# Second half of a 16-expert layer: down products from one fp32 product to three passes on split operands

## What is computed

```python
weights, indices = _gate(x2, Wg)          # four of sixteen experts for a token
for e in range(16):
    we = jnp.sum(weights * (indices == e), axis=-1)
    h = silu(x2 @ W1[e].T + b1[e]) * (x2 @ W3[e].T + b3[e])
    y = y + (h @ W2[e].T + b2[e]) * we[:, None]
x = x + tanh(g_ffn[2]) * y
```

## Time and profile before

| | |
|---|---|
| median of 3 runs (lowest, highest) | 599.43 us (598.75, 601.22) |
| the profiled execution's own time | 601.89 us |
| its span from first to last instruction | 600.1 us |
| busy in the span: PE, DVE, ACT, POOL | 94%, 75%, 69%, 17% |
| share of PE on the chain that ended last | 71% |
| layer 2's loop of 32 steps, in the span | 387.2 to 449.5 us |

### The profile page before, as it was taken

The page is one execution under the profiler, slowest core; times in us unless marked ns, Lnnn a source line. Parts: engine busy times, 40 slices in busy tenths (PEclk is TensorE's granted clock), DMA queues, the critical chain, the costliest instruction groups (busy, mean ns, idle before and its releaser), DMA issues.

```text
span 600.1 us, 8818 instructions
## 1 busy us (share of the span) xinstructions
PE 566.8 (94%) x3305; PEld 394.1 (66%) x3310; DVE 447.4 (75%) x696; ACT 415.2 (69%) x579; POOL 103.8 (17%) x69
## 2 busy tenths in 40 slices
PE   7999999989999999999896989999998999999997
PEld 5688787656677777775230436566545777888886
DVE  4378987588657898987989676766766847787786
ACT  4798999756755556647999765534513858888885
POOL 5400000001200000003989703200000210000000
PEclk9999999999999999999999799999998999999999
DMA  6207210200200811020000024505510110812100
GB/s 237 71 12 307 71 35 2 74 2 2 76 0 4 317 55 58 2 70 1 5 1 1 1 71 120 164 2 153 163 35 2 37 37 0 301 52 72 37 0 35
DMA packets 16782, 40.27 MB, mean 67 GB/s; under 512 B 1834, under 2 KB 6058, under 8 KB 16740
## 3 DMA queue, kind: packets, MB, share of 16 engines
q1 hardware_dynamic: 16740, 39.71, 19.9%
HBM read 39.01 MB, written 0.70 MB: 66 GB/s over the span
## 4 chain that ended last, share of the span: by engine, by line
PE 71%; DVE 14%; ACT 10%; issue 3%; POOL 1%; DVEq 0%; ACTq 0%; POOLq 0%
PE ps L713 38%; ACT work L1094 6%; PE ps L756 4%; PE ps L452 3%; DVE h_lo L1609 2%; PE ps L469 2%; PE ps L739 2%; PE ps L584 2%; PE ps L741 2%; PE ps L555 2%; PE ps L740 2%; PE ps L569 2%; PE ps L459 2%; PE ps L695 2%; DVE h_act L1586 1%
## 5 line engine op out<-in xcount | busy, mean ns | idle before, releaser
L1609 DVE TENSOR_TENSOR h_lo<-h_act,h_hi 128x512 fp32r<-128x512 f32 (+1 forms) x136 | 118.4, 874 | 39.8 <-ACT h_hi L1139 39.0
L713 PE MATMUL ps<-n_hi,w_hi 128*128 128x512 f32 (+1 forms) x232 | 85.4, 402 | 2.0 <-DVE h_act L1586 1.3
L1139 ACT CAST h_hi<-h_act 128x1024 fp32r<-128x1024 f32 (+1 forms) x88 | 75.3, 856 | 14.6 <-PE ps L713 12.1
L713 PE MATMUL ps<-n_hi,w_lo 128*128 128x512 f32 (+1 forms) x232 | 83.0, 391 | 0.0
L713 PE MATMUL ps<-n_lo,w_hi 128*128 128x512 f32 (+1 forms) x232 | 83.0, 391 | 0.0
L1817 POOL TENSOR_TENSOR rstd<-var_eps,minus_half 128x4 f32<-128x4 f32 x16 | 17.5, 1093 | 319.4 <-DVE var_eps L1273 319.4
L713 PE MATMUL ps<-h_hi,w_hi 128*128 128x512 f32 (+1 forms) x184 | 65.5, 398 | 0.1
L713 PE MATMUL ps<-h_hi,w_lo 128*128 128x512 f32 (+1 forms) x184 | 64.0, 390 | 0.0
L713 PE MATMUL ps<-h_lo,w_hi 128*128 128x512 f32 (+1 forms) x184 | 63.9, 389 | 0.0
L1094 ACT ACTIVATE work<-work,p_rest 128x2048 f32<-128x2048 f32 x31 | 59.5, 1998 | 0.4 <-DVE work L1468 0.4
L1132 ACT ACTIVATE h_act<-ps 128x512 f32<-128x512 f32 (+1 forms) x48 | 28.6, 596 | 40.4 <-PE ps L713 40.4
(11 more groups left out here) (234 smaller groups left out, 1023.7 us busy)
## 6 DMA issues: line engine op xcount, KB each, us to landing
work<-g_rows SPq DMA_DIRECT2D x36, 512.0 KB, 6.4
w_f<-in_w SPq DMA_DIRECT2D x20, 512.0 KB, 3.6
w_f<-in_w SPq DMA_DIRECT2D x8, 544.0 KB, 3.6
work<-in_w SPq DMA_DIRECT2D x2, 512.0 KB, 4.3
work<-g_rows SPq DMA_DIRECT2D x4, 256.0 KB, 9.7
p_rest<-in_p_rest SPq DMA_DIRECT2D x1, 714.0 KB, 9.8
p_attn<-in_p_attn SPq DMA_DIRECT2D x1, 546.5 KB, 6.9
x<-in_xT SPq DMA_DIRECT2D x1, 512.0 KB, 3.6
```

The lines of the kernel that those rows point to most:

```text
L713: mm = pe.matmul(dst[i], wap(wt, e, lo, size, rows), mv[i], start=(first and c == 0), stop=(last and c == 2))
L1139: act.copy(places(h_hi, m, step), places(h_act, m, step)).then_inc(s["hi"], 1)
L1609: dve.tensor_tensor(lo, src, hi.bitcast(F32), ALU.subtract).then_inc(s["lo"], 1)
```

## The change

The downs of steps 16 to 31 (`t == 1`) are made as the ups are: three passes on split operands in place of one fp32 product. For that, ACT rounds each scaled result to a high part (`high2`, one CAST of 128 x 512), DVE subtracts to get the low part (`low2`), and W2 is split in four pieces of four experts each (`split_hi_down2` on ACT, `split_lo_down2` on DVE). The parts of steps 16 to 25 have two buffers, taken in turn (`spare` for the high part, the first halves of `n_hi` and `n_lo` for the low part), so `high2(step)` waits for down step - 2; steps 26 to 29 have four more in `h_hi`, `h_lo`, and steps 30, 31 take the first two again.

`ahead_of` now goes one up for two downs from step 3 on, until four ups are ahead, and then one for one. DVE's products follow `products2`. Where the other work stands is changed too: the norm's mean, variance, spread and the queries after downs 20, 23, 26 and 29; its square and copy on ACT inside the loop; the key copies at ACT's steps 18 and 19; the keys spread one piece a step. The small `uv_line` is now a piece of `h_act`.

```diff
     def ahead_of(self, step):
+        if self.layer == 2:
+            return min(max(min(step + self.ahead + 1, 18 + max(step - 3, 0) // 2), step + 5), self.total)
...
+        def h2_split(step):
+            if 26 <= step < 30:
+                return [flat(h)[:, (step - 26) * HALF:(step - 25) * HALF] for h in (h_hi, h_lo)]
+            return spare[:, half(step % 2)], (n_hi, n_lo)[step % 2][:, 0:HALF]
+        def products2(step):
+            m = MOES[2]
+            return min(m.ahead_of(step) - (2 if step < 8 else 3) if step < 27 else step + 3, m.total)
...
-                        pe.wait_ge(s["scaled"], step + 1)
-                        pe.matmul(ps[:, acc + t], down2(e), h_part[step % 16], start=False, stop=(step + 1 == m.last_of(t))).then_inc(s["h_used"], 1)
+                        if t == 0:
+                            pe.wait_ge(s["scaled"], step + 1)
+                            mm = pe.matmul(ps[:, acc], down2(e), h_part[step % 16], start=False, stop=(step + 1 == m.last_of(t)))
+                        else:
+                            pe.wait_ge(s["lo"], step - 15)
+                            if e % 4 == 0:
+                                pe.wait_ge(s["wld"], e // 4 + 1)
+                            hi, lo = h2_split(step)
+                            pe.matmul(ps[:, acc + 1], down2_half(w_hi, e), hi, start=False, stop=False)
+                            pe.matmul(ps[:, acc + 1], down2_half(w_hi, e), lo, start=False, stop=False)
+                            mm = pe.matmul(ps[:, acc + 1], down2_half(w_lo, e), hi, start=False, stop=(step + 1 == m.last_of(t)))
+                        mm.then_inc(s["h_used"], 1)
...
+                def high2(step):
+                    act.wait_ge(s["scaled"], step + 1)
+                    if step < 26:
+                        act.wait_ge(s["h_used"], step - 1)
+                    else:
+                        act.wait_ge(s["hid"], 2 * (step - 13) if step < 30 else m.total)
+                        act.wait_ge(s["h_used"], 26)
+                    act.copy(h2_split(step)[0], h_part[step % 16]).then_inc(s["hi"], 1)
...
+                        if step == 27:
+                            norm_square(6, 0)
+                            norm_copy(6, 0)
+                        for ready in range(16, m.total):
+                            if min(products2(min(ready + 1, m.total - 1)), m.total - 1) == step:
+                                high2(ready)
...
+                def low2(step):
+                    dve.wait_ge(s["hi"], step - 15)
+                    dve.tensor_tensor(h2_split(step)[1], h_part[step % 16], h2_split(step)[0].bitcast(F32), ALU.subtract).then_inc(s["lo"], 1)
...
-                        if step + 12 < m.total:
+                        while len(made) < products2(step):
                             ahead()
                         scale(step)
+                        if step >= 17:
+                            low2(step - 1)
+                        if step in (11, 15, 19, 23):
+                            split_lo_down2((step - 11) // 4)
```

More of the change, by code:

```diff
@@ L143, in flamingo @@
         uv = sb("uv", [P, 2, S])
-        uv_line = sb("uv_line", [2, T])
+        spare = sb("spare", [P, T], F32R)
         uv_rows = nc.dram_tensor("uv_rows", (2, T), F32, kind="Internal").ap()
@@ L153, in flamingo @@
         h_lo = sb("h_lo", [P, 2, T], F32R)
+        uv_line = h_act[0:2, 0]
         g_sb = sb("g_sb", [P, 2, T])
@@ L242, in up2_lo, with down2_half, four, down2_four @@
             return cols(w_lo if e < 8 else flat(h_lo), e, 2 * P)
+        def down2_half(w, e):
+            return w[:, e * P:(e + 1) * P]
+        def four(w, g):
+            return w[:, 4 * g * P:4 * (g + 1) * P]
+        def down2_four(g):
+            return (w_f32[:, T + g * HALF:T + (g + 1) * HALF] if g < 2 else diag[:, (g - 2) * HALF:(g - 1) * HALF])
+        def h2_split(step):
[5 more added lines that the diff above has]
+            return min(m.ahead_of(step) - (2 if step < 8 else 3) if step < 27 else step + 3, m.total)
         def down2(e):
@@ L266, in flamingo @@
         mo = [{k: sem(f"m{m.layer}_{k}") for k in ["hid", "act", "h_used", "whu", "wlu"] + ["mul"] * m.gated
-              + ["wlu_first"] + (["scaled", "sel"] if m.layer == 2 else ["hi", "lo", "whd", "wld", "wld_first", "gate", "acc"]) + ["xn"] * (m.layer == 3)} for m in MOES]
+              + ["wlu_first"] + (["scaled", "sel", "hi", "lo", "whd", "wld"] if m.layer == 2 else ["hi", "lo", "whd", "wld", "wld_first", "gate", "acc"]) + ["xn"] * (m.layer == 3)} for m in MOES]
         w_in = [[sem(f"w{m.layer}_in{u}") for u in range(m.slots if m.layer != 2 else 0)] for m in MOES]
@@ L903, in _ @@
             moe(MOES[1], {42: [lambda: norm_mean(4, 0)], 43: [lambda: norm_var(4, 0)], 44: [lambda: norm_spread(4, 0)], 46: [first_features]})
-            moe(MOES[2], {19: [lambda: norm_mean(6, 0)], 21: [lambda: norm_var(6, 0)], 24: [lambda: norm_spread(6, 0)], 28: [lambda: queries(1, 0)]})
+            moe(MOES[2], {20: [lambda: norm_mean(6, 0)], 23: [lambda: norm_var(6, 0)], 26: [lambda: norm_spread(6, 0)], 29: [lambda: queries(1, 0)]})
             attention(1)
@@ L1146, in high, with split_hi_down2 @@
                     act.copy(h_hi[0:size, (step % 4) // 2, half(step % 2)], src).then_inc(s["hi"], 1)
+                def high2(step):
[6 more added lines that the diff above has]
+                    act.copy(h2_split(step)[0], h_part[step % 16]).then_inc(s["hi"], 1)
+                def split_hi_down2(g):
+                    act.wait_ge(w2_down_in[g // 2], 16)
+                    act.copy(four(w_hi, g), down2_four(g)).then_inc(s["whd"], 1)
                 def copy_gates(t=0):
@@ L1161, in moe @@
                 if L == 2:
+                    act.wait_ge(pre["uv_dram"], 16)
                     copy_gates(0)
@@ L1193, in moe @@
                             copy_gates(1)
-                        if step in (19, 22):
-                            copy_keys(1, 1, (step - 19) // 3)
-                        for t in range(2):
-                            if step - 23 - 5 * t in (0, 1):
-                                for h in range(2):
-                                    expand_keys(1, t, 2 * (step - 23 - 5 * t) + h)
+                        if step in (18, 19):
+                            copy_keys(1, 1, step - 18)
+                        if step in (17, 20, 22, 24):
+                            split_hi_down2((17, 20, 22, 24).index(step))
+                        if 20 <= step < 28:
+                            expand_keys(1, (step - 20) // 4, step % 4)
+                        if step == 27:
[4 more added lines that the diff above has]
+                                high2(ready)
                     load_table(ACT.Exp)
-                    norm_square(6, 0)
-                    norm_copy(6, 0)
                     query_rows(1, 0)
@@ L1598, in scale, with split_lo_down2 @@
                     dve.tensor_tensor(h, h, g_half[:, e], ALU.mult).then_inc(s["scaled"], 1)
+                def low2(step):
+                    dve.wait_ge(s["hi"], step - 15)
+                    dve.tensor_tensor(h2_split(step)[1], h_part[step % 16], h2_split(step)[0].bitcast(F32), ALU.subtract).then_inc(s["lo"], 1)
+                def split_lo_down2(g):
+                    dve.wait_ge(s["whd"], g + 1)
+                    dve.tensor_tensor(four(w_lo, g), down2_four(g), four(w_hi, g).bitcast(F32), ALU.subtract).then_inc(s["wld"], 1)
                 def low(step):
@@ L1648, in moe @@
                 if L == 2:
-                    steps = itertools.count()
+                    made = []
                     def ahead():
-                        product(next(steps))
+                        made.append(len(made))
+                        product(made[-1])
                     def add(t):
@@ L1692, in moe @@
                             add(0)
+                    low2(m.total - 1)
                     query_rows(1, 0)
@@ L1804, in _ @@
             pair_sums()
[L1805 removed]
+            moe(MOES[2], {**rotations(1, 4), 24: [lambda: norm_eps(6, 0)], 28: [lambda: norm_out(6, 0)]})
             attention(1)
```

5 lines of the change are left out of this document (2 added, 3 removed).

## The result

The changed kernel takes 616.6 us (median of five executions, 615.5 to 621.2), the kernel before 599.3 us beside it. The ratio is 1.029, with a 95% interval of 1.026 to 1.032. A sixth execution of the changed kernel was disturbed (1950.61 us) and is left out of all of this; with it the median would be 618.2. The profiled execution took 619.72 us for a span of 617.9, against 601.89 and 600.1.

A forecast was written before the change was run, and what follows sets the result against it. PE was taken to bound layer 2. Savings (-2.1 + 0.7 - 0.4) and 15.5 us of waits made 13.7; with 1.5 for the clock, +15.2 on 599.4 gave 614.6 us, range 607.5 to 620.

The forecast's parts named there:

- up 24: Second half: PE waits 2.3 us for product 22, behind rounding, low part and sum that follow down 15.
- Saved: Up to the queries: thirteen downs at 0.70 us in place of 0.86, -2.1; down 29 adds 0.7; a 0.44 gap goes.
- up 20: PE waits 1.2 us for product 18, which stands behind DVE's key turn and ACT's second key copy.
- up 25: PE waits 1.7 us for product 23, behind low part 19, whose rounding waits for down 17's buffer.
- the variance: Layer norm: PE waits 1.4 us for ACT's square, which stands behind hidden 27 and a spread of keys.
- downs 26 and 27: Loop's end: each right behind an up (30, 31) that its high and low parts hang on; 2.2 us wait each.
- down 29: Last down ahead of the queries: a wait of 0.5 us at the loop's end.
- The walk: Stepping through the new in-order engine lists with the old trace's prices, noting PE's waits: 15.5 us; queries 13.7 us later.
- The clock: In the stretch with ten gaps, one fall of PE's clock, counted at 1.5 us; none and three were the ends.
- The rival with several falls: Layer 2's loop: the clock falls three times or more, +18.2 us and up, 617.6 to 622 us; chance 0.14.
- PE does not wait: Rival for the whole loop: engines run far enough ahead; 1.8 us less, 597.6 us; chance 0.06.
- Only the end waits: Rival: places 1 to 4 of the waits vanish, 6.7 us at the end stay; +4.9, 604.3 us; chance 0.08.

The follow-up runs named there:

- e4: e1's order, unsplit, with the second half's downs in three passes on operands that lie ready, so no rounding or subtraction for them; 604.1 us, 1.008 of the kernel before.
- e10: e8 with another searched order, GpSimd's power and hand-overs counted longer, and the first two roundings waiting for no down; 596.8 us, 0.9945 of the kernel before.
- e9: The kernel before, nothing split, with its PE, ACT and DVE lists from down 3 to the scores put in a searched order; 598.3 us, 0.996.
- e1: The changed kernel's order with nothing split: all down products single fp32 products, no roundings or low parts; 606.8 us, 1.012 of the kernel before.
- e6: The changed kernel with the ups running five steps ahead of the downs in the second half in place of four; 612.4 us, 1.018 of the kernel before.
- e8: The changed kernel's split and two buffers, with PE, ACT and DVE lists from down 3 in a searched order and some waits freed; 597.4 us, 0.995 of before.
- e2: The changed kernel with idle products on PE ahead of its longest waits, no wait taken away; 615.0 us, 1.024 of the kernel before.
- e7: The changed kernel with a third buffer for high parts of steps 16 to 25, roundings 26 to 29 not waiting for down 25; 615.6 us, 1.026 of before.

## Why the prediction held, and where it was off

The time lay in the range (607.5 to 620), 2.0 us above the forecast of 614.6; one of the five executions, 621.2, lies above the range. Two terms of the sum were off, in opposite directions: the waits were somewhat smaller than forecast, and the clock cost more.

**What bounds, and the prices.** Held. Two downs of three passes start 0.70 us apart; the five ups that waited for DVE started 0.05 or 0.06 us after their product's record ended, and not the 0.15 of the earlier trace rows. But behind such a first pass the next one starts 0.33 us later and not 0.23, so what a hand-over costs PE is some 0.15 after all. For up 24 (the weight load is engine PEld):

```profile
423.66 0.19 PEld L763 LDWEIGHTS ps<-n_hi,h_hi 128*128 128x128 f32 x1 [2.49 <-DVE y_g L1639]
423.99 0.39 PE L764 MATMUL ps<-n_lo,h_hi 128*128 128x512 f32 x1
424.22 0.40 PE L765 MATMUL ps<-n_hi,h_lo 128*128 128x512 f32 x1
```

The row is no clean price of a product's hand-over: the weight load of that up waited too, and the profile puts it down to GpSimd, which made the weights' low part.

```profile
385.67 0.19 PEld L739 LDWEIGHTS ps<-n_hi,h_hi 128*128 128x128 f32 x1 [0.89 <-POOL h_lo L1833]
```

The Trainium skill (TensorE: Matmul & The Clock Gate, section "Architectural detail: the array is 16× 32×32, not 1× 128×128") says that PE's queue can pull weight loads ahead of running matmuls. At this hand-over the trace does not show it: the first weight load of up 24 stands at 423.66 with its pass, and not in the 2.06 us of wait ahead of it.

**Saved.** 0.16 us for a down were forecast, 2.6 for the sixteen in the stretch. PE's work there is less by 2.2 us (the estimate above), in e4, where the clock did not fall, by 2.3, and in e10 against e9, where nothing waits, by 2.9. Held.

**Added waits.** The places were right, all but the last: up 20 1.2 forecast and 1.14 measured; up 24 2.3 and 2.06; up 25 1.7 and 0.87, up 26 0.8 and 0.60; the variance 1.4 and 1.00, up 28 1.2 and 0.91; downs 26 and 27 2.2 each and 2.01 each; down 28 1.8 and 1.49; down 29 0.5 and none. The walk counts a wait from where PE is free, the profile from the end of the record, which is 0.16 us later; so 2.06 stands against 2.3 as 2.22, and the nine waits, 12.1 us as measured, come to some 13.5 against the 15.5 of the sum. The largest miss is up 25. Just ahead of it and of down 29 PE was at its lower clock, and its slower work would lie over the wait; that is argued and not tested apart. That the order makes the waits was argued; e1 (this order without the split), e6 (another lead) and e8 (another order, some waits freed) show it, and the waits go where the walk says, but for the two of e8.

**The clock.** This is the term that was mis-sized most. It was counted as one fall and 1.5 us; the profiled execution has four in the stretch, 8.5 us of full-speed work. The argument was that a gap of 1.65 us had left the clock alone. In the changed kernel it fell behind waits of 2.06, 0.91, 2.01 and 2.01 us, and not behind that of 1.14 at 409.01. So one row of a gap without a fall is no protection: the first fall came behind the second wait of the loop already. The rival with several falls, given a chance of 0.14 and 617.6 to 622 us, is what the profiled execution did, on top of the forecast's mechanism; two of the five executions lie in its range, and three, the median among them, in the forecast's own (611 to 617.5). e2 is the forecast nearly to the letter: the same places, one fall, 615.0 us. Not all that the falls withhold is lost time: e2's stretch is 4.5 us shorter than the changed kernel's, for 6.8 us less withheld, and in the medians it is 1.6. That, the smaller waits and the 1.6 us behind the scores are why the time came out nearer to the forecast than 8.5 us against 1.5 would suggest; that these offset each other in part is luck.

The Trainium skill (TensorE: Matmul & The Clock Gate, "Part 1: The HAM clock gate (the "warmup" mystery)") has the throttled clock as the default, which activity releases. The trace agrees in that the clock fell behind waits or inside them (0.50 to 0.81 in the windows above), and stood at 1.00 in the stretches of e9 and e10, where PE hardly waits. For two executions of five in that rival's range, the chance of 0.14 was small.

**The rivals.** PE does not wait: false for this order, and what e10 does in another. Only the end waits: false; the first six waits are there, 6.6 us in all.

What stays open: when the clock falls. It fell behind a wait of 0.91 us, which followed one of 1.00, and not behind one of 1.14 that stood alone; but in e4 the same two places have 1.20 and 0.91 and the clock stayed at 1.00, while in e1 and e7 it fell there. And how much of the split's gain would show in the whole time, since e8, e9 and e10 can't be told apart there; by the stretch it is 2.6 us (e10 against e9).

## What to carry to other kernels

A split that takes a little work from the engine that bounds and gives more to two that have room is decided by the order of the hand-overs: here the same instructions took 617 us in one order and 597 in another, in which some of their waits could be freed. So walk the new lists with the prices of the old trace before building, put each rounding and low part one or two steps ahead of its consumer, and never a consumer right behind the last instruction that its operand needs. Where a walk finds many waits on TensorE, leave room for the clock to fall at several of them: with six to ten waits it fell from none (e4) to four times here, and not equally often in each execution. And look whether the same search makes the old kernel faster too, since here a third of the gain needed no split.

## What the runs showed of the hardware that was not expected

GpSimd's power on 128 x 4 numbers, the same instruction each time, took 1.01 us in the changed kernel and in e10, 1.40 before and 2.59 in e8. The timelines of GpSimd and of DVE at that time, first e8:

```profile
434.49 2.59 POOL L1897 TENSOR_TENSOR rstd<-var_eps,minus_half 128x4 f32<-128x4 f32 x1 [51.70 <-DVE var_eps L1346]
...
434.33 0.68 DVE L1671 TENSOR_TENSOR vblk<-vblk,work 128x512 f32<-128x512 f32 x1
434.93 1.29 DVE L1675 TENSOR_TENSOR h_lo<-kT,h_hi 128x512 fp32r<-128x512 f32 x2
436.13 0.74 DVE L1659 SCALAR_TENSOR_TENSOR vblk<-ps,p_rest,vblk 128x512 f32<-128x512 f32 x1
```

and e10:

```profile
432.05 1.01 POOL L1899 TENSOR_TENSOR rstd<-var_eps,minus_half 128x4 f32<-128x4 f32 x1 [49.61 <-DVE var_eps L1348]
...
431.88 0.74 DVE L1661 SCALAR_TENSOR_TENSOR vblk<-ps,p_rest,vblk 128x512 f32<-128x512 f32 x1
```

In e8 the power fell on three DVE instructions with both inputs in SBUF, and ended 0.95 us after DVE came to one that reads PSUM; in e10 it began beside one that reads PSUM and had no delay. The Trainium skill (SBUF — State Buffer, section "SBUF: two separate sides") says that GpSimd and a VectorE instruction with two SBUF inputs take turns at a shared port pair, each for a whole instruction. These rows fit that; GpSimd then did not come in between any two of the three in e8. But before, four such instructions of DVE stood in a row from 438.17 on the earlier trace rows, and the power took 1.40 us beside them:

```profile
438.33 1.40 POOL L1817 TENSOR_TENSOR rstd<-var_eps,minus_half 128x4 f32<-128x4 f32 x1 [52.90 <-DVE var_eps L1273]
...
438.78 1.29 DVE L1598 TENSOR_TENSOR txt<-txt,work 128x512 f32<-128x512 f32 x2
```

There it ended while the third of them was running. So a run of such instructions does not by itself hold GpSimd up to its end; why it did in e8 stays open, and no run here tests it apart. The profile's spans on GpSimd are rough; that of e8 is borne out by PE, whose spread product starts at 437.13, 0.05 us behind its end.
